# Root, column sums and turns of the identity in the first two pairs of an attention pipeline

## Chip, cores, metric

One NeuronCore of a Trainium2 chip runs the whole program. The metric is the device time of one execution in microseconds, the median of several runs. The trace is that of one profiled execution; its times count from the start of its span.

## What is computed

A batch of 32 images (3 x 128 x 128) and 32 texts (128 tokens) goes through two layers at width 256; only the first layer matters here. Cut to it:

```python
img = einsum(patches16x16(x), W) + b            # 64 image tokens per batch element
txt = take(weight, x_txt)                        # 128 text tokens
h   = concat(img, txt)                           # [32, 192, 256]
n   = layernorm(h)
q, k, v = n @ wq.T, n @ wk.T, n @ wv.T
h   = h + softmax(causal(q @ k.T / 16)) @ v
n2  = layernorm(h)
h   = h + ternary(gelu(ternary(n2, w_up)), w_down)
# ternary(x, w): x / (rms(x) + eps) times w_t.T, where w_t is sign(w) where |w| > 0.5 * mean|w|, else 0
```

The second layer (a gated linear recurrence and a mixture of eight experts) follows and is not touched.

## The kernel before

The first layer works on pairs of batch elements, 16 pairs, n = 0 to 15; a pair is 3 tiles of 128 tokens. All products are f32 made from a high part in the rounded type that TensorE takes and a low remainder, so most operands are split: ScalarE or VectorE copies the high part, VectorE or GpSimd subtracts it to get the low part. `product(..., three(...))` sums high x high, high x low and low x high. The ternary weights are exact and need no split.

The work of one pair is cut into pieces with names, and one list, `order`, gives the sequence of the pieces. Each engine walks through this same list in each step g and does the part of a piece that is its own. `offset` says which pair a piece works on in step g: pieces of offset 2 (tok, emb, root1, apply1, xT, x_split, t, t_split, score, max, and also merge and tern_up) work on pair g+2, those of offset 1 (exp, pT, v, pv, h1, scale2, x2T, also abs_down and tern_down) on pair g+1, up, gelu and down on pair g, patch_split and gather on pair g+3, patch_load on pair g+4. Steps -4 to 1 are written out before the loop, so pair 0 runs tok to max in step -2 and exp to x2T in step -1, where pair 1 runs its tok to max; the first up and down products come in step 0. Semaphores order the engines; an engine's queue is in order.

The pieces of the first half, with what each does:

- patch_split: VectorE casts `patches` to `pat_h` (`patch_hi`, for pairs 0 and 1 called from other places, for pair 1 at the end of emb of pair 0), GpSimd subtracts to `pat_l` (L333). patch_load on SyncE waits for both before it loads the next pair's patches into the single buffer.
- tok: 18 products of 256 columns from the patches and the token weights (loaded in chunks and split on the way in).
- merge (pair 0 only): folds wq and wk into one matrix; qk_split splits it.
- emb: VectorE adds the bias, takes `bn_stats` and `bn_aggr` of three tiles. root1: GpSimd adds epsilon and takes the power -0.5. apply1: VectorE norms x (L625).
- xT: six TensorE transposes; x_split: ScalarE high, VectorE low. t: 12 products of 384 columns; t_split likewise; score: 18 products of 256 columns; max: masks and takes row maxima.
- exp, pT, v (18 products), pv (15 products), h1, root2, scale2, x2T (six transposes), x2_split.

The conversion of the ternary weights runs once, inside these steps: `abs_sum(n)` sums the absolute values of the raw weights on VectorE (n = 0 up, n = 1 down), a product with a matrix of ones on TensorE sums over the partitions (its result is alpha), and `ternary(n)` scales alpha and then makes two halves of 1024 columns in two VectorE instructions each:

```python
if g == -2:
    abs_sum(0)                                   # VectorE, ahead of emb of pair 0
if kind in ("merge", "tern_down") and n == 0:    # TensorE
    pe.wait_ge(s["w_abs"], q + 1); matmul(ps[:, 7, q:q + 1], ones, absum[:, q:q + 1])
```

abs_down stands behind apply1, tern_up behind x_split, tern_down behind t_split. up of pair 0 waits for the up weights, down for the down weights.

PSUM has eight banks: XT in 0 and 1, t and the scores (and tok) in 2 and 3, v and pv in 4 and 5, up and down in 6 and 7, alpha in a column of 7. `ident` is the identity matrix, made by GpSimd before the first layer's block.

Of the kernel before, what the change touches and what calls it, by code (L numbers as in the profile page):

```python
# [18 lines left out]
ALU = mybir.AluOpType  # L19
ACT = mybir.ActivationFunctionType  # L20
F32 = mybir.dt.float32
# [5 lines left out]
P = 128  # L27
# [44 lines left out]
def part_a(nc, W, io, consts):  # L72
    with ExitStack() as ctx:
# [74 lines left out]
        for src, hi, lo in ((io["tokW"], tok_h, tok_l), (io["wvT"], wv_h, wv_l)):  # L148
            cols = flat(hi).shape[1]
            for a in range(0, cols, 1024):  # L150
# [10 lines left out]


        order = """ids_load exp gelu_table tok merge pT up.0 up.1 patch_split patch_load emb pT_split root1 gelu.0 gelu.1 v
                v_split apply1 qk_split abs_down up.2 up.3 gelu.2 add.1 up.4 pv gelu.3 add.2 xT gelu.4 up.5 x_split tern_up
                gelu.5 up.6 add.3 up.7 gelu.6 gelu.7 exp_table t h1 root2 gather t_split tern_down add.4 add.5
                down.0 down.1 score scale2 add.6 add.7 x2T down.2 max ss x2_split rscale
                h2.0 h2.1 h2.2""".split()
        order = [(w.split(".")[0], int((w + ".0").split(".")[1])) for w in order]
        offset = {"turn_win": 0, "fold": 0, "up": 0, "gelu": 0, "add": 0, "down": 0, "ss": 0, "rscale": 0, "h2": 0, "tok": 2, "emb": 2, "root1": 2, "apply1": 2,
# [117 lines left out]
        @block.gpsimd  # L287
        def _(pool):

            nc.gpsimd.memset(mask[:], 0.0).then_inc(s["mask_zero"], 1)  # L290
            pool.wait_ge(s["mask_zero"], 1)
            nc.gpsimd.affine_select(out=mask[:, 0, :], in_=mask[:, 0, :], compare_op=ALU.is_ge, fill=MASKED,
                                    base=0, pattern=[[-1, D]], channel_multiplier=1).then_inc(s["mask_zero"], 1)
            pool.wait_ge(s["mask_zero"], 2)

            nc.gpsimd.affine_select(out=mask[:, 0, 0:N_IMG], in_=mask[:, 0, 0:N_IMG], compare_op=ALU.is_ge,
                                    fill=MASKED, base=N_IMG - 1, pattern=[[0, N_IMG]],
                                    channel_multiplier=-1).then_inc(s["mask_zero"], 1)

            nc.gpsimd.memset(mask[:, 1, N_IMG:2 * N_IMG], MASKED)  # L300
            nc.gpsimd.memset(mask[:, 2, 0:N_IMG], MASKED)
            nc.gpsimd.affine_select(out=mask[:, 1:3, P:2 * P], in_=mask[:, 1:3, P:2 * P], compare_op=ALU.is_ge,
                                    fill=MASKED, base=0, pattern=[[0, 2], [-1, P]],
                                    channel_multiplier=1).then_inc(s["mask_ready"], 1)

            def gather(n, sl, half):
                pool.wait_ge(ids_in[sl], 16 * (half + 1))
                wait(pool, s["h1_done"], n - 1)
                settle(pool)
                for j in range(2):  # L310
                    pool.indirect_dma_start(
                        emb[:, sl, 1 + j, :], None, io["table"],
                        bass.IndirectOffsetOnAxis(ap=ids[:, sl, j:j + 1], axis=0),
                    ).then_inc(text_in[sl], 16)

            def prepare(g):
                if g == -4:
                    gather(0, 0, 0)

            def piece(kind, k, n, sl, half):  # L320
                if kind == "gather" and not (isinstance(n, int) and n == 0):
                    gather(n, sl, half)
                if kind == "gelu" and k in lo_pool and not (isinstance(n, int) and n == G - 1 and k in last_lo_vector):

                    if k in hi_scalar:
                        pool.wait_ge(s["ffn_hi_s"], len(hi_scalar) * n + hi_scalar.index(k) + 1)
                    else:
                        pool.wait_ge(s["ffn_hi"], (FC - len(hi_scalar)) * n + k + 1)
                    nc.gpsimd.tensor_tensor(act_l[:, k, :], act[:, k % DEEP, :], act_h[:, k, :].bitcast(F32),  # L329
                                            ALU.subtract).then_inc(s["ffn_lo"], 1)  # L330
                if kind == "patch_split":
                    pool.wait_ge(s["patch_hi"], n + 1)
                    nc.gpsimd.tensor_tensor(pat_l[:], patches[:], pat_h[:].bitcast(F32),  # L333
                                            ALU.subtract).then_inc(s["patch_lo"], 1)
                if kind == "root1":
                    pool.wait_ge(s["ln_aggr"], n + 1)
                    settle(pool)
                    nc.gpsimd.tensor_scalar(ve[:], moments[:, :, 1], LN_EPS, None, ALU.add).then_inc(s["ln_ve"], 1)
                    pool.wait_ge(s["ln_ve"], n + 1)
                    wait(pool, s["ln_out"], n)  # L340
                    nc.gpsimd.tensor_tensor(rstd[:], ve[:], halfpow[:, 1, 0:TILES], ALU.pow).then_inc(s["ln_rstd"], 1)
                if kind == "rscale":

                    pool.wait_ge(s["ms_done"], n + 1)
                    wait(pool, s["rden_done"], n)
                    nc.gpsimd.tensor_tensor(rms[:], ms[:], halfpow[:, 0, 0:TILES], ALU.pow).then_inc(s["rms_done"], 1)
                if kind == "root2":
                    pool.wait_ge(s["ln2_aggr"], n + 1)
                    settle(pool)
                    nc.gpsimd.tensor_scalar(pair[:, 0, :], moments2[:, :, 1], 0.0, None, ALU.add)  # L350
                    nc.gpsimd.tensor_scalar(pair[:, 1, :], moments2[:, :, 1], LN_EPS, None,
                                            ALU.add).then_inc(s["ln2_pair"], 1)
                    pool.wait_ge(s["ln2_pair"], n + 1)
                    nc.gpsimd.tensor_tensor(roots[:], pair[:], halfpow[:, 0:1, 0:TILES].to_broadcast([P, 2, TILES]),
                                            ALU.pow).then_inc(s["ln2_roots"], 1)

            run(pool, piece, prepare)
# [96 lines left out]
        def _(v):  # L454
# [5 lines left out]
                v.wait_ge(s["w_abs_parts"], n + 1)  # L460
                nc.vector.tensor_reduce(absum[:, n:n + 1], abparts[:], AX_X, ALU.add).then_inc(s["w_abs"], 1)

            def ternary(n):
                raw, out = raw_tern[n], tern[n][2]
                v.wait_ge(s["w_alpha_ps"], n + 1)
                nc.vector.tensor_scalar(half_alpha[:, n:n + 1], ps[:, 7, n:n + 1], 0.5 / (D * FF), None,
                                        ALU.mult).then_inc(s["w_alpha"], 1)
                v.wait_ge(s["w_alpha"], n + 1)

                for part in range(2):  # L470
                    col = slice(1024 * part, 1024 * part + 1024)
                    k = 2 * n + part
                    wait(v, s["w_sum"], k)
                    nc.vector.tensor_scalar(tern_tmp, raw[:, col], -1.0, half_alpha[:, n:n + 1], ALU.mult,
                                            ALU.is_gt).then_inc(s["w_sign"], 1)
                    v.wait_ge(s["w_sign"], k + 1)
                    last = nc.vector.scalar_tensor_tensor(out=out[:, col], in0=raw[:, col],
                                                          scalar=half_alpha[:, n:n + 1], in1=tern_tmp,
                                                          op0=ALU.is_gt, op1=ALU.subtract)
                    last.then_inc(s["w_sum"], 1)  # L480

            def softplus_arg():
                omega = vec[:, 0, :]
# [29 lines left out]
            def prepare(g):  # L513
# [6 lines left out]
                for n in chunks_of.get(g, ()):  # L520
                    chunk_lo(n)
                if g == -2:
                    abs_sum(0)
                    v.wait_ge(s["const_in"], 16)
                    v.wait_ge(s["mask_ready"], 1)

# [15 lines left out]
            def piece(kind, k, n, sl, half):  # L542
# [24 lines left out]
                    nc.vector.tensor_tensor(sqsum[:], sqsum[:], sq[:, k % DEEP, :], ALU.add).then_inc(s["sqsum_done"], 1)  # L567
                if kind == "x_split":
                    lo(xT_l[:], XT[:, :, 0:GT], xT_h[:].bitcast(F32), s["x_hi"], s["x_lo"], n)
                if kind == "t_split":  # L570
                    lo(tT_l[:], ps[:, 2:4, 0:GT], tT_h[:].bitcast(F32), s["t_hi"], s["t_lo"], n)
                if kind == "v_split":
# [16 lines left out]
                if kind == "abs_down" and isinstance(n, int) and n == 0:  # L589
                    abs_sum(1)  # L590
                if kind in ("tern_up", "tern_down") and isinstance(n, int) and n == 0:
                    ternary(("tern_up", "tern_down").index(kind))
                if kind == "max":
                    v.wait_ge(s["score_done"], n + 1)
                    wait(v, s["pT_done"], n)
# [86 lines left out]
        def _(pe):  # L682
# [16 lines left out]
            def keys(x, k, i):  # L699
# [2 lines left out]
                    return x[:, k, 0:2 * P]  # L702
                return x[:, k, :].rearrange("p (t c) -> p t c", t=TILES)[:, 0:3:2, :]

            def piece(kind, k, n, sl, half):
                if kind == "merge" and isinstance(n, int) and n == 0:
                    pe.wait_ge(s["qk_in"], 32)
                    for m in range(DC):
# [1 line left out]
                            last = nc.tensor.matmul(MERGED[:, m, :], wq[:, c, m * P:(m + 1) * P], wk[:, c, :],  # L710
                                                    start=(c == 0), stop=(c == DC - 1))
                    last.then_inc(s["merge_ps"], 1)
                if kind in ("merge", "tern_down") and isinstance(n, int) and n == 0:
                    q = ("merge", "tern_down").index(kind)
                    pe.wait_ge(s["w_abs"], q + 1)
                    nc.tensor.matmul(ps[:, 7, q:q + 1], ones[:], absum[:, q:q + 1], start=True,
                                     stop=True).then_inc(s["w_alpha_ps"], 1)
# [962 lines left out]
```

## Time and profile before

| | |
|---|---|
| median of 3 runs | 1002.25 us (1001.86 to 1004.44) |
| profiled execution | 1003.52 us, its span 1001.5 us |
| TensorE busy | 932.3 us (93%) |
| VectorE busy | 786.3 us (79%) |
| ScalarE busy | 594.7 us (59%) |
| GpSimd busy | 542.3 us (54%) |
| mean granted TensorE clock | 0.974 |

The span is what the profile covers; the execution's own time is 2.0 us longer. In the profile PE is TensorE's matrix products, PEld its weight loads, DVE VectorE, ACT ScalarE, POOL GpSimd and SP SyncE. An instruction's row names the line of the kernel, the output and the inputs. Several products of a form that follow each other stand in one row with their count. Matrix products overlap in their pipeline, so each one's duration is longer than the distance to the next. The granted clock (PEclk) is a share of the full 2.4 GHz: 1.00 or 0.50.

### The profile page before, as it was taken

The numbers are of one execution on the slowest core, as the hardware profiler recorded it, in microseconds if no ns is written. First come the engines' busy times: TensorE is split into PE (matmuls) and PEld (weight loads), VectorE is DVE, ScalarE is ACT, GpSimd is POOL, SyncE is SP. The second block draws the span as 40 slices with busy tenths as digits, with TensorE's granted clock in tenths as the row PEclk, the third lists the DMA queues.
The fourth block names the chain that finished last, engine by engine and source line by source line (L and its number), as shares of the span: only waits on it lengthen the run. The fifth ranks groups of instructions, "written<-read, shape, count | busy, mean of one in ns | idle before, by whom it ended". The sixth has DMA issues, their size and how long they took to land. (4 is left out here: it accounts for less than half of the span.)

```text
span 1001.5 us, 19582 instructions
## 1 busy us (share of the span) xinstructions
PE 932.3 (93%) x5896; PEld 834.9 (83%) x5896; DVE 786.3 (79%) x2396; ACT 594.7 (59%) x1181; POOL 542.3 (54%) x662
## 2 busy tenths in 40 slices
PE   3779999999999999988799999999998999997998
PEld 2679999999999999875588888888887788886887
DVE  3578777777777777774399999999997888996776
ACT  1246666666666666664566677767664676652541
POOL 4136666666666666443445555445443446542663
PEclk9679999999999999999899999999999899999999
DMA  6001111111111113003699999999999999994210
GB/s 214 22 27 44 43 44 35 50 36 47 39 45 34 50 33 148 17 17 111 79 149 155 157 155 154 156 155 155 153 153 177 146 151 150 140 143 78 102 63 22
DMA packets 135877, 96.33 MB, mean 96 GB/s; under 512 B 12270, under 2 KB 130166, under 8 KB 135158
## 3 DMA queue, kind: packets, MB, share of 16 engines
q1 hardware_dynamic: 134262, 91.20, 53.0%
q0 software_dynamic: 1536, 4.20, 1.4%
q8 instruction: 35, 0.57, 0.3%
q14 instruction: 44, 0.36, 0.2%
HBM read 31.91 MB, written 13.11 MB: 45 GB/s over the span
## 5 line engine op out<-in xcount | busy, mean ns | idle before, releaser
L329 POOL TENSOR_TENSOR gelu_lo<-gelu_out,gelu_hi 128x384 fp32r<-128x384 f32 x124 | 145.4, 1200 | 30.0 <-DVE gelu_hi L548 28.7
L1025 POOL TENSOR_TENSOR B_y<-B_scan_in,B_states 128x512 f32<-128x512 f32 x48 | 61.9, 1289 | 97.9 <-ACT B_states L1099 97.9
L741 PE MATMUL psAB<-ternary_down,gelu_hi 128*128 128x256 f32 x384 | 96.6, 290 | 4.8 <-POOL gelu_lo L329 3.9
L685 PE MATMUL psAB<-x2T_hi,ternary_up 128*128 128x384 f32 x256 | 93.2, 364 | 2.5 <-DVE residual L675 2.3
L741 PE MATMUL psAB<-ternary_down,gelu_lo 128*128 128x256 f32 x384 | 93.3, 282 | 0.0
L685 PE MATMUL psAB<-x2T_lo,ternary_up 128*128 128x384 f32 x256 | 86.2, 337 | 0.0
L1273 PE MATMUL psAB<-Win_hi,B_x_hi 128*128 128x512 f32 x192 | 83.5, 435 | 0.0
L1285 PEld LDWEIGHTS psAB<-B_partial_dots,B_minus_same_batch 128*128 128x128 f32 x384 | 65.3, 191 | 17.9 <-DVE B_partial_dots L1176 8.9
L741 PEld LDWEIGHTS psAB<-ternary_down,gelu_hi 128*128 128x128 f32 x384 | 72.2, 188 | 8.8 <-POOL gelu_lo L329 7.5
L1192 DVE SCALAR_TENSOR_TENSOR psAB<-B_decayed_u,psAB 128x128 f32<-128x128 f32 x192 | 67.9, 354 | 13.4 <-PE psAB L1285 12.1
L1273 PE MATMUL psAB<-Win_hi,B_x_lo 128*128 128x512 f32 x192 | 75.7, 394 | 0.0
L1273 PE MATMUL psAB<-Win_lo,B_x_hi 128*128 128x512 f32 x192 | 75.1, 391 | 0.0
L1037 POOL TENSOR_TENSOR B_decayed_u<-B_scan_in 128x512 f32<-128x512 f32 x48 | 62.0, 1292 | 24.2 <-DMA B_scan_in<-B_stage 14.0
L741 PEld LDWEIGHTS psAB<-ternary_down,gelu_lo 128*128 128x128 f32 x384 | 72.4, 189 | 0.0
L1031 POOL TENSOR_TENSOR B_v_scale<-B_half_vv,half_powers 128x1 f32<-128x1 f32 x48 | 26.3, 548 | 83.6 <-ACT B_v_squared L1120 77.5
L1176 DVE CUSTOM_DVE_ANT_0 B_products<-B_scan_in,psAB 128x128 f32<-128x128 f32 x192 | 55.1, 287 | 18.7 <-DVE psAB L1192 7.8
L398 ACT ACTIVATE gelu_out<-psAB 128x384 f32<-128x384 f32 x128 | 62.8, 491 | 10.9 <-PE psAB L685 10.3
L333 POOL TENSOR_TENSOR patches_lo<-patches,patches_hi 128x768 fp32r<-128x768 f32 x16 | 29.5, 1847 | 65.7 <-DVE patches_hi L536 65.6
L1181 DVE TENSOR_TENSOR psAB<-psAB,B_scan_in 128x128 f32<-128x128 f32 x192 | 57.5, 299 | 6.5
L567 DVE TENSOR_TENSOR gelu_sq_sum<-gelu_sq_sum,gelu_sq 128x384 f32<-128x384 f32 x105 | 61.2, 583 | 1.7
L1285 PE MATMUL psAB<-B_partial_dots,B_minus_same_batch 128*128 128x1 f32 x384 | 55.0, 212 | 7.0 <-DVE B_partial_dots L1176 6.8
L685 PEld LDWEIGHTS psAB<-x2T_hi,ternary_up 128*128 128x128 f32 x256 | 48.0, 188 | 11.8 <-ACT gelu_out L398 7.7
(265 smaller groups left out, 3345.2 us busy)
## 6 DMA issues: line engine op xcount, KB each, us to landing
B_scan_in<-B_stage SPq DMA_DIRECT2D x192, 256.0 KB, 6.6
patches<-in_patches SPq DMA_DIRECT2D x16, 384.0 KB, 3.1
B_residual<-layer_out SPq DMA_DIRECT2D x48, 128.0 KB, 3.6
out_dram<-B_residual SPq DMA_DIRECT2D x48, 128.0 KB, 2.9
layer_out<-residual SPq DMA_DIRECT2D x32, 128.0 KB, 1.8
raw_Win<-in_experts SPq DMA_DIRECT2D x4, 768.0 KB, 4.4
raw_Wl<-in_experts SPq DMA_DIRECT2D x4, 768.0 KB, 4.2
layer_out<-residual SPq DMA_DIRECT2D x32, 64.0 KB, 1.9
```

What stands on the lines that cost most here:

```text
L329: nc.gpsimd.tensor_tensor(act_l[:, k, :], act[:, k % DEEP, :], act_h[:, k, :].bitcast(F32), ALU.subtract).then_inc(s["ffn_lo"], 1)
L398: nc.scalar.activation(act[:, k % DEEP, :], ps[:, 6 + k % 2, 0:GT], ACT.Gelu).then_inc(s["gelu_done"], 1)
L567: nc.vector.tensor_tensor(sqsum[:], sqsum[:], sq[:, k % DEEP, :], ALU.add).then_inc(s["sqsum_done"], 1)
L685: last = nc.tensor.matmul(out, a, b, start=(n == 0), stop=(n == len(terms) - 1))
L741: last = nc.tensor.matmul(ps[:, 6 + k // 2, (k % 2) * D:(k % 2 + 1) * D], x[:, c, k * P:(k + 1) * P], dn_w[:, c, :], start=(c == 0 and x i ...
L1025: nc.gpsimd.tensor_tensor(y[:, j % 2], ring[:, j % R_RING, :, GATE, :], hs[:, j % 2], ALU.mult).then_inc(s["y"], 1)
L1037: nc.gpsimd.tensor_tensor(lu[:, j % 2], ring[:, j % R_RING, :, LAM, :], ring[:, j % R_RING, :, U, :], ALU.mult).then_inc(s["lu"], 1)
L1176: nc.vector.tensor_tensor_reduce(prod[:], ring[:, j % R_RING, k, U, :], previous(j, k), 1.0, 0.0, ALU.mult, ALU.add, part[:, t % 2:t % 2 + ...
L1181: nc.vector.tensor_tensor(state(j, k), state(j, k), ring[:, j % R_RING, k, DRIVE, :], ALU.subtract).then_inc(s["scan"], 1)
L1192: nc.vector.scalar_tensor_tensor(out=state(i, k), in0=lu[:, i % 2, k, :], scalar=dot[:, t % 2:t % 2 + 1], in1=state(i, k), op0=ALU.mult, o ...
L1273: last = nc.tensor.matmul(out, a, b, start=(not biased and ks[0] == 0 and n == 0), stop=(ks[-1] == DC - 1 and n == len(terms) - 1), skip_g ...
L1285: nc.tensor.matmul(dot[:, t % 2:t % 2 + 1], minus[:], part[:, t % 2:t % 2 + 1], start=True, stop=True).then_inc(s["dot"], 1)
```

## The change

It touches the first pairs only.

- On GpSimd the low part of pair 1's patches moves from the piece patch_split to behind the root of pair 0.
- On VectorE `abs_sum(0)` moves from the start of step -2 to behind x_split of pair 0, and TensorE's alpha product for the up weights from merge to t_split, in front of which it waits for the column sums.
- `ternary` makes one half per call. The halves are tern_up.0 behind t_split, tern_up.1 behind max, tern_down.0 and tern_down.1 behind t_split in their step.
- TensorE transposes the identity into PSUM bank 6, which nobody reads then, a number of times ahead of the wait of eight pieces: 110 times in all. A piece's turns stand before all that the piece does on TensorE, its waits included.

```diff
-                v_split apply1 qk_split abs_down up.2 up.3 gelu.2 add.1 up.4 pv gelu.3 add.2 xT gelu.4 up.5 x_split tern_up
-                gelu.5 up.6 add.3 up.7 gelu.6 gelu.7 exp_table t h1 root2 gather t_split tern_down add.4 add.5
-                down.0 down.1 score scale2 add.6 add.7 x2T down.2 max ss x2_split rscale
+                v_split apply1 qk_split abs_down up.2 up.3 gelu.2 add.1 up.4 pv gelu.3 add.2 xT gelu.4 up.5 x_split
+                gelu.5 up.6 add.3 up.7 gelu.6 gelu.7 exp_table t h1 root2 gather t_split tern_up.0 tern_down.0 tern_down.1 add.4 add.5
+                down.0 down.1 score scale2 add.6 add.7 x2T down.2 max tern_up.1 ss x2_split rscale
...
+            def patch_lo(n):
+                pool.wait_ge(s["patch_hi"], n + 1)
+                nc.gpsimd.tensor_tensor(pat_l[:], patches[:], pat_h[:].bitcast(F32),
+                                        ALU.subtract).then_inc(s["patch_lo"], 1)
...
-                if kind == "patch_split":
-                    pool.wait_ge(s["patch_hi"], n + 1)
-                    nc.gpsimd.tensor_tensor(pat_l[:], patches[:], pat_h[:].bitcast(F32),
-                                            ALU.subtract).then_inc(s["patch_lo"], 1)
+                if kind == "patch_split" and not (isinstance(n, int) and n == 1):
+                    patch_lo(n)
...
                     nc.gpsimd.tensor_tensor(rstd[:], ve[:], halfpow[:, 1, 0:TILES], ALU.pow).then_inc(s["ln_rstd"], 1)
+                    if isinstance(n, int) and n == 0:
+                        patch_lo(1)
...
-            def ternary(n):
+            def ternary(n, part):
...
                 if g == -2:
-                    abs_sum(0)
...
                 if kind == "x_split":
                     lo(xT_l[:], XT[:, :, 0:GT], xT_h[:].bitcast(F32), s["x_hi"], s["x_lo"], n)
+                    if isinstance(n, int) and n == 0:
+                        abs_sum(0)
...
+            fill = {("tok", 0): 40, ("xT", 0): 16, ("t", 0): 10, ("score", 0): 10, ("pv", 0): 10, ("xT", 1): 4,
+                    ("t", 1): 10, ("score", 1): 10}
+
             def piece(kind, k, n, sl, half):
+                if isinstance(n, int):
+                    for _ in range(fill.get((kind, n), 0)):
+                        nc.tensor.transpose(ps[:, 6, 0:P], ident[:], ident[:])
...
-                if kind in ("merge", "tern_down") and isinstance(n, int) and n == 0:
-                    q = ("merge", "tern_down").index(kind)
+                if kind in ("t_split", "tern_down") and isinstance(n, int) and n == 0 and k == 0:
+                    q = ("t_split", "tern_down").index(kind)
```

## Rows read from the trace of the kernel before

**Rows 1.** The page, granted TensorE clock in 40 slices of 25 us, in tenths.

```profile
PEclk9679999999999999999899999999999899999999
```

**Rows 2.** Windows over the run: length, each engine's busy us and instructions, PEclk, DMA.

```profile
0.00:100.00 100.00, 70.19 (x418) 66.57 (x419) 62.41 (x150) 38.20 (x75) 41.40 (x53) 0.83 0.23 77
100.00:200.00 100.00, 99.04 (x734) 95.86 (x733) 78.45 (x224) 64.69 (x136) 69.38 (x68) 1.00 0.15 43
```

**Rows 3.** What TensorE waited for, 0 to 70 us: total, times, longest.

```profile
PE psAB L685 <- DVE tokW_lo L530: 10.9, 1, 10.9
PE psAB L696 <- DVE x_normed L625: 6.3, 1, 6.3
PE psAB L685 <- DVE xT_lo L540: 3.8, 2, 1.9
PE psAB L685 <- DVE tT_lo L540: 3.6, 2, 1.9
PE psAB L685 <- DVE v_lo L540: 2.0, 1, 2.0
```

**Rows 4.** Windows, L685's products alone: tok(0), t(0), score(0), tok(1), v(0), t(1) twice.

```profile
10.90:15.10 4.20, 4.18 (x18) 1.00 1.03 430
26.90:31.20 4.30, 4.21 (x12) 0.50 0.00 0
33.00:37.30 4.30, 4.21 (x18) 0.50 0.00 0
38.60:42.65 4.05, 3.96 (x18) 0.50 0.01 4
43.00:45.50 2.50, 2.29 (x18) 1.00 0.00 0
51.90:52.85 0.95, 0.89 (x5) 1.00 0.00 0
52.85:55.50 2.65, 2.59 (x9) 0.50 0.00 0
```

**Rows 5.** Windows, all engines: PE, PEld, DVE, ACT, POOL, PEclk, DMA.

```profile
22.10:22.30 0.20, 0.00 (x0) 0.00 (x0) 0.00 (x0) 0.00 (x0) 0.20 (x1) 0.58 0.10 31
...
49.50:52.90 3.40, 1.51 (x11) 1.27 (x10) 3.04 (x6) 2.30 (x3) 0.00 (x0) 0.99 0.00 0
...
63.20:66.50 3.30, 3.23 (x15) 3.23 (x16) 2.02 (x9) 1.65 (x5) 0.00 (x0) 0.50 0.00 0
```

**Rows 6.** Timeline, VectorE and GpSimd, 14 to 23.5 us: start, us, instruction, idle before.

```profile
14.27 2.29 DVE L458 TENSOR_REDUCE abs_sum_parts<-raw_Wl 128x32 f32<-128x2048 f32 x1 [3.51 <-DMA raw_Wl<-in_upT]
...
16.71 0.42 DVE L607 TENSOR_TENSOR embedded<-psAB,patch_bias 128x256 f32<-128x256 f32 x1
...
18.65 0.53 DVE L536 CAST patches_hi<-patches 128x768 fp32r<-128x768 f32 x1
19.25 1.80 POOL L333 TENSOR_TENSOR patches_lo<-patches,patches_hi 128x768 fp32r<-128x768 f32 x1 [10.18 <-DVE patches_hi L536]
...
21.47 0.90 POOL L341 TENSOR_TENSOR ln_rstd<-ln_var_eps,half_powers 128x3 f32<-128x3 f32 x1
22.41 1.06 DVE L625 TENSOR_SCALAR x_normed<-embedded,ln_moments,ln_rstd 128x256 f32<-128x256 f32 x3 [3.23 <-POOL ln_rstd L341]
```

**Rows 7.** Tile patches, 0 to 20 us: its two loads, issued at 2.4 and 9.1.

```profile
DMA to landing us min/median/max: 3.2/5.9/8.6
```

**Rows 8.** Timeline, VectorE, 56 to 63.5 us.

```profile
56.32 0.96 DVE L540 TENSOR_TENSOR tT_lo<-psAB,tT_hi 128x768 fp32r<-128x768 f32 x1 [1.70 <-ACT tT_hi L374]
...
60.56 1.28 DVE L477 SCALAR_TENSOR_TENSOR ternary_down<-raw_Wv,half_alpha,gelu_sq 128x1024 fp32r<-128x1024 f32 x1
...
62.16 1.06 DVE L668 TENSOR_SCALAR x_normed<-residual,ln_moments,ln_scale 128x256 f32<-128x256 f32 x3
```

**Rows 9.** Timeline, TensorE: the six transposes of xT(0) and of xT(1).

```profile
23.52 1.54 PE L696 MATMUL psAB<-ident,x_normed 128*128 128x128 f32 x6 [6.31 <-DVE x_normed L625]
...
49.25 0.82 PE L696 MATMUL psAB<-ident,x_normed 128*128 128x128 f32 x6
```

More of the change, by code:

```diff
@@ L461, in abs_sum @@
                 nc.vector.tensor_reduce(absum[:, n:n + 1], abparts[:], AX_X, ALU.add).then_inc(s["w_abs"], 1)
-            def ternary(n):
+            def ternary(n, part):
                 raw, out = raw_tern[n], tern[n][2]
[L465 to L480, printed above, removed]
+                if part == 0:
+                    v.wait_ge(s["w_alpha_ps"], n + 1)
+                    nc.vector.tensor_scalar(half_alpha[:, n:n + 1], ps[:, 7, n:n + 1], 0.5 / (D * FF), None,
+                                            ALU.mult).then_inc(s["w_alpha"], 1)
+                    v.wait_ge(s["w_alpha"], n + 1)
+                col = slice(1024 * part, 1024 * part + 1024)
+                k = 2 * n + part
+                wait(v, s["w_sum"], k)
+                nc.vector.tensor_scalar(tern_tmp, raw[:, col], -1.0, half_alpha[:, n:n + 1], ALU.mult,
+                                        ALU.is_gt).then_inc(s["w_sign"], 1)
+                v.wait_ge(s["w_sign"], k + 1)
+                nc.vector.scalar_tensor_tensor(out=out[:, col], in0=raw[:, col], scalar=half_alpha[:, n:n + 1],
+                                               in1=tern_tmp, op0=ALU.is_gt, op1=ALU.subtract).then_inc(s["w_sum"], 1)
             def softplus_arg():
@@ L591, in piece @@
                 if kind in ("tern_up", "tern_down") and isinstance(n, int) and n == 0:
-                    ternary(("tern_up", "tern_down").index(kind))
+                    ternary(("tern_up", "tern_down").index(kind), k)
                 if kind == "max":
```

## The prediction

> **What bounds the kernel now.** I read four views, from coarse to fine. The forty slices of the page show TensorE's granted clock near full almost everywhere, and low in the second and third slice [rows 1]. The windows over the run say the same in time: after 100 us TensorE is busy 99 of 100 us at the full clock, in the first 100 us it is busy 70 us at a mean of 0.83 [rows 2]. So behind the first steps the kernel is bound by TensorE, and what the first steps save should arrive at the end one for one: nothing else paces the loop, and the loop's own work isn't changed. TensorE's waits in the first 70 us name the chain of the first two pairs: 10.9 us for the low part of the token weights, 6.3 for the first normed x, 3.8 and 3.6 for the low parts of xT and tT of both pairs [rows 3]. These are steps that follow each other with nothing to put between.
>
> The fourth view is the clock inside this head. The engine has two levels, 1.2 and 2.4 GHz. The same eighteen 256-wide products take 4.2 us in the score of pair 0, and 2.29 us in v of pair 0 [rows 4], a ratio of 0.54. The clock column says 1.00 for tok of pair 0, yet its duration (4.18 us for eighteen) is that of half clock: before the first recorded change I go by durations. The column then shows a fall at 22.2 us, after TensorE had stood idle since 17 (its 6.3 us ahead of xT at 23.5 [rows 3]); half clock through t and score of pair 0 and through tok of pair 1; full clock from 42.6; half again from 52.9, after a stretch in which it was busy only 1.5 of 3.4 us; and a return in 66.5, at the end of 3.2 us without a pause [rows 4, 5]. t and score of pair 0 are each 4.2 us of unbroken products, with 1.8 us between them, and did not raise it.
>
> **The change, part by part.**
>
> *Root ahead of the split, column sums behind x's split.* In the kernel before, VectorE holds the patch-bias add until 16.71 us, because it sums the columns of the raw ternary weights from 14.27 on for 2.3 us and a short second reduction follows; the product it needs was ready at 15.1 [rows 4, 6]. Then the statistics end at about 18.65, VectorE casts the patches of pair 1 (0.53 us), and GpSimd first takes their low part from 19.25 to 21.05. Only then does the variance go to the root: 0.90 us from 21.47, and x is normed from 22.41 [rows 6].
> After the change the add starts when tok is done: 15.1 at half clock, 13.3 if tok runs at full clock. Statistics take 1.94 us as before (16.71 to 18.65), so they end at 17.1 or 15.3. The variance add and root then need 1.4 us (from 21.05 to 22.4), so rstd is there at 18.5 or 16.7. But the cast of the patches of pair 1 stays ahead of x's norming on VectorE, and their load was issued at 9.1 and landed 8.6 us later, at 17.7 [rows 7], behind the weights. Nothing in the change moves that load. So the cast ends at about 18.3, and norming starts at 18.3 to 18.5 at either clock: **-4.0 us** (-3.9 to -4.1). The queue behind the cast is VectorE's; on GpSimd the low split and the gather of pair 1 now follow the root, at about 20.1 instead of 21.05, and the load of the next patches goes out that much earlier, so nothing waits longer.
>
> *The column sums' new place.* Behind xT's low part they take 2.3 + 0.2 us of VectorE. The next thing it owes is tT's low part, which waits for t (4.2 us at half, 2.3 at full clock) and for ScalarE's copy: of the 1.8 us from t's end to the score's start the low part itself is 0.96 [rows 4, 8], so the copy some 0.8. Cover 3.1 us at the least, cost 0. If the cover were gone it would be up to 2.5. The alpha product on TensorE now waits for them after t: they end 2.6 us after xT's low part, t at full clock 2.3 us after it, and 1.8 us of wait follow anyway: cost 0.
>
> *Ternary halves.* In pair 1 the two halves of the down weights stand between tT's low part (ends 57.28) and 61.84, so a half is 2.3 us with its gaps and its share of the scaling [rows 8]. The first up half takes as much of VectorE between tT's low part and the row maxima; the score covers it with 2.3 us at full clock plus its start and end: cost **+0.1**. The second stands after the maxima, under tok of pair 1: 0. The down halves keep their place. Behind them the second norm goes from 62.16 to 63.22: from 56.3 on that stretch is VectorE's, so a faster score of pair 1 gives **0**.
>
> *The identity turns.* A 128-wide transpose of f32 takes (1.54 - 0.48)/5 = 0.21 us at half and (0.82 - 0.27)/5 = 0.11 us at full clock, where 0.48 and 0.27 are what one takes by itself, an estimate; six of them are 1.54 and 0.82 [rows 9]. The 40 ahead of tok: 8.5 us at the most, inside the 10.9 us of wait. 16 ahead of xT(0): 1.8 to 3.4 us, from about 15 on, ready before 19.4. 10 ahead of t, score and pv: 1.1 us at full clock in waits of 1.9, 1.8 and 2.0: free; at half clock 2.1, and with the alpha product in front score(0) and score(1) come 0.6 us late each. The 4 ahead of xT(1) stand in no wait: pv(0) runs until 49.25, where xT(1) starts at once [rows 9], so they cost **+0.4** (0.9 at half).
>
> What they give is the clock, if they raise it. This is the step I can't read off a row, so I bound it. Nothing: the clock rises as products alone make it. Everything: full clock from before tok(0) to the end of the head. Then xT(0) 1.54 to 0.82: **-0.7**; t(0) 4.2 to 2.3: **-1.9**; score(0) the same: **-1.9**; tok(1) 3.96 to 2.29: **-1.7** (v of pair 0 and pv were at full clock already); t(1) 0.89 + 2.59 to 2.3: **-1.2**; x2T the same 0.7 as xT, and 0.3 of tok(2), whose rest I take as hidden under the exponentials of pair 1: **-1.0** [rows 4, 9].
> Do transposes wake the clock? The row that bears on it is 63.2 to 66.5: it begins with the six transposes of x2T (1.1 us of the 3.2), and the clock rose at its end, while 4.2 us of products with a pause behind them did not raise it [rows 4, 5]. So I take it that they count nearly like products. The Trainium skill says otherwise (TensorE: Matmul & The Clock Gate, Part 4: PE-mode transpose): by it the full clock doesn't engage for transposes, since they don't count as busy in the same way. The trace speaks against it, with that one stretch. By the rule the sum would be that of the second rival.
>
> Sum with the full clock throughout: -4.0 - 0.7 - 1.9 - 1.9 - 1.7 - 1.2 - 1.0 + 0.1 + 0.4 = **-11.9**. It won't be throughout. Between the 16 turns (done by about 16.7) and xT at 19.4 TensorE stands still for 2.7 us, and a longer still stretch from 17 made it fall before: I give back xT's 0.7 and a third of t, +1.3. Between score(1), which ends near 60 at full clock, and x2T at 63.3 on the old scale lie 3.3 us without a turn: I give back the last term, +1.0. Likeliest: -11.9 + 2.3 = **-9.6 us**.
>
> The sum was made on the profiled execution (span 1001.5, 1003.5 with 2.0 around it), which is 1.3 us above the median of 1002.25. The same saving from the median: 1002.25 - 9.6 = **992.6 us**; a profile after should have a span near 992.
>
> **The rivals.**
> 1. *Clock up throughout*: 1002.25 - 11.9 = 990.4. For it: the waits are filled densely. Against: the two unfilled ones above.
> 2. *Transposes don't wake the clock.* Only the root's part is left, and the turns run at half clock: -4.0 + 0.6 + 0.6 + 0.4 + 0.1 = -2.3, so 999.9. Against it speaks the stretch at 63.2.
> 3. *The clock falls in the gap ahead of xT(0) and comes back only in tok(1).* Then xT(0), t(0), score(0) and half of tok(1) stay at half clock, the turns of the score cost 0.6: of -11.9 + 1.0 are lost 0.7 + 1.9 + 1.9 + 0.9 + 0.6 = 6.0; left is -4.9, so 997.3. For it: VectorE's wait for the patches makes this gap, and the fall at 22.2 is a precedent; against: 10 turns fill the wait right behind xT.
> 4. *No change*: a head start that the loop doesn't keep, because its first steps wait for something with its own time, a gather or a load: 1002. Against: both are issued earlier too, and after 100 us TensorE is 99% busy.
> 5. *Slower.* The rise at 42.6 is lost: it came out of 4.0 us of tok(1) [rows 4]. If the turns neither raise the clock nor keep it and tok(1) starts at another moment, v(0), pv(0) and xT(1) run at half clock too: +1.9, +1.6, +0.7, t(1)'s first half +0.5, the four turns +0.5 more, pv's turns +0.2; on -2.3 that is +3.1, so 1005.4. It decides only if transposes count for nothing and this rise is missed as well.
>
> **How the numbers follow.** Forecast 0.55, rival 1 0.11, rival 3 0.15, rival 2 0.12, rival 4 0.05, rival 5 0.02. 0.3% is 3.0 us, about what this measurement can tell from no change. The forecast and rivals 1 and 3 are faster beyond it (0.81); rival 2 at -2.3 us lies just inside, with 0.05 of its 0.12 beyond: faster 0.86, the same 0.07 + 0.05 = 0.12, slower 0.02. The range goes from 989.0, 1.4 under rival 1 for its rounded terms, to 998.5, 1.2 over rival 3: it leaves out rivals 2, 4 and 5, 0.19.
>
> **What the profile after would show.** The patch-bias add at 13.3 (15.1 if the 40 turns didn't raise the clock), VectorE idle ahead of the cast of pair 1's patches until 17.7 with a DMA as releaser, norming at 18.3. Score(0)'s eighteen products in 2.3 us and not 4.2. Norming of pair 1 some 9 us earlier, x2T near 54, the products of the first ternary layer starting near 58.5. A short low of the granted clock around 18 to 23 us and another near 52. The prediction is wrong if products behind the turns last as long as at half clock, if norming waits for something later than the patches, or if TensorE shows new waits between 60 and 100 us.

## The result and the profile after

| | before | after |
|---|---|---|
| median of 9 runs each | 1004.44 us (1001.56 to 1007.69) | 995.29 us (992.05 to 999.17) |
| ratio | | 0.9916, 95% interval 0.9898 to 0.9935 |
| profiled execution, its span | 1003.52 us, 1001.5 us | 999.17 us, 997.4 us |

The change makes the kernel 0.84% faster by the ratio, which is 8.4 us (the two medians lie 9.2 apart). The prediction was 992.6 us (989.0 to 998.5), 9.6 us less than the median it started from. The profiled execution after is the slowest of its nine, and its span is only 4.1 us shorter; where the other half went is read further down.

The windows over the run of the kernel after, with the columns of [rows 2]:

```profile
0.00:100.00 100.00, 83.92 (x580) 79.67 (x581) 70.02 (x165) 45.00 (x89) 48.95 (x61) 0.97 0.23 77
100.00:200.00 100.00, 99.20 (x736) 96.06 (x735) 78.87 (x224) 64.70 (x135) 68.94 (x67) 1.00 0.15 43
```

TensorE's mean clock in the first 100 us is 0.97 where it was 0.83 (the column reads 1.00 ahead of the first recorded change in both, so both means are somewhat high); the loop behind it is as it was. TensorE's waits of 0 to 70 us, which answer to [rows 3]:

```profile
PE psAB L699 <- DVE x_normed L628: 4.6, 1, 4.6
PE psAB L699 <- DVE x_normed L671: 3.2, 1, 3.2
...
PE psAB L688 <- DVE tokW_lo L531: 1.6, 1, 1.6
PE psAB L688 <- DVE tT_lo L541: 1.0, 2, 0.6
PE psAB L688 <- DVE v_lo L541: 0.9, 1, 0.9
PE psAB L688 <- DVE xT_lo L541: 0.8, 1, 0.8
```

The waits that have turns in them shrank, though the work behind them starts no earlier for that. Two are long: 4.6 us ahead of xT(0), and 3.2 us ahead of x2T(0), which was 1.7 and now has the end of a faster score in front of it.

The windows of the products alone (columns of [rows 4]) are tok(0), t(0), score(0), tok(1), t(1), score(1) and tok(2):

```profile
10.90:13.35 2.45, 2.39 (x18) 1.00 1.01 413
24.70:27.20 2.50, 2.38 (x12) 0.97 0.02 3
29.00:31.50 2.50, 2.42 (x18) 1.00 0.00 0
32.80:35.30 2.50, 2.38 (x18) 1.00 0.00 0
...
44.90:47.35 2.45, 2.38 (x12) 1.00 0.00 0
49.10:51.65 2.55, 2.41 (x18) 1.00 0.00 0
55.90:59.70 3.80, 3.71 (x18) 0.60 0.00 0
```

All five blocks that ran wholly or partly at half clock in [rows 4] take 2.4 us now, as at full clock; score(1), which has no row there, is too. tok(2), which has none either, is at 0.60: the clock fell at 55.5, just behind the wait of 3.2 us, and came back at 59.0.

TensorE's transposes in time, the turns (L716, out psAB, in ident) and xT's (L699); [rows 9] are those of before:

```profile
2.00 7.37 PE L716 MATMUL psAB<-ident 128*128 128x128 f32 x40 [2.00 <-PEq L1609]
...
14.88 1.91 PE L716 MATMUL psAB<-ident 128*128 128x128 f32 x16
21.35 1.51 PE L699 MATMUL psAB<-ident,x_normed 128*128 128x128 f32 x6 [4.55 <-DVE x_normed L628]
22.66 2.32 PE L716 MATMUL psAB<-ident 128*128 128x128 f32 x10
...
41.76 0.60 PE L716 MATMUL psAB<-ident 128*128 128x128 f32 x4
42.20 0.82 PE L699 MATMUL psAB<-ident,x_normed 128*128 128x128 f32 x6
```

The 40 turns take 7.37 us: all at half clock would be 8.5, all at full 4.5, so the clock rose among them, and tok(0) behind them ran at full clock. The windows say roughly when: 26 turns in the 5.4 us up to 7.4, then 15 (with those that reach in) in 1.8 us. Turn by turn the trace has them 0.21 us apart up to the one that starts at 7.8, and 0.11 apart from there on.

```profile
2.00:7.40 5.40, 5.40 (x26) 5.40 (x27) 0.75 (x1) 1.27 (x2) 4.20 (x9) 1.00 0.70 223
...
7.60:9.40 1.80, 1.76 (x15) 1.52 (x13) 0.95 (x1) 0.92 (x2) 1.49 (x1) 1.00 0.99 351
```

TensorE had done nothing but turns of the identity until then. Transposes wake the clock in this kernel. (The Trainium skill, TensorE: Matmul & The Clock Gate, Part 4: PE-mode transpose, says that they don't; the trace differs, and the measurement decides.) The clock column itself says 1.00 from the start here as in the kernel before, so the distances between instructions show this rise and the column doesn't.

VectorE and GpSimd, 13 to 21 us, which answer to [rows 6]:

```profile
13.46 0.42 DVE L610 TENSOR_TENSOR embedded<-psAB,patch_bias 128x256 f32<-128x256 f32 x1 [2.68 <-PE psAB L688]
...
18.25 0.56 DVE L537 CAST patches_hi<-patches 128x768 fp32r<-128x768 f32 x1 [2.77 <-DMA patches<-in_patches]
18.73 2.56 DVE L628 TENSOR_SCALAR x_normed<-embedded,ln_moments,ln_rstd 128x256 f32<-128x256 f32 x3
...
16.00 0.90 POOL L344 TENSOR_TENSOR ln_rstd<-ln_var_eps,half_powers 128x3 f32<-128x3 f32 x1
18.89 1.91 POOL L318 TENSOR_TENSOR patches_lo<-patches,patches_hi 128x768 fp32r<-128x768 f32 x1 [1.99 <-DVE patches_hi L537]
```

The add starts at 13.46 (predicted 13.3), the root is ready at 16.9 (16.7), VectorE waits 2.77 us for the load of pair 1's patches as foretold, and norming starts at 18.73 (18.3), because the load landed 9.1 us after its issue here and not 8.6 as before. But norming takes 2.56 us instead of 1.06. Its three instructions, in the view of the tile (ns, min/median/max):

```profile
L628 DVE TENSOR_SCALAR x_normed<-embedded,ln_moments,ln_rstd x3: 409/426/1893, 18.7 to 20.9; 128x256 f32<-128x256 f32 x3
```

The one of 1893 ns started behind GpSimd's low part (18.89 to 20.80) and ended 0.15 us behind its end: VectorE stood inside an instruction, which no view of waits shows.

**Where the profile's other 4 us are.** up of pair 0 starts at 59.98 instead of 68.07, so the head gained 8.1 us in the profiled execution too. At pT of pair 15 the lead is still there, 409.80 instead of 417.98. In both executions two stalls of 1.2 and 0.6 us stand there (the kernel after):

```profile
409.80 0.74 PE L826 MATMUL psAB<-ident,probs 128*128 128x128 f32 x5 [1.21 <-DVE x2T_lo L541]
411.16 0.69 PE L688 MATMUL psAB<-x2T_hi,ternary_up 128*128 128x384 f32 x1 [0.62 <-DVE residual L678]
411.65 0.52 PE L688 MATMUL psAB<-x2T_lo,ternary_up 128*128 128x384 f32 x1
```

Behind them the products are 0.32 us apart, as at half clock; in the kernel before they are 0.17 apart behind the same stalls. The windows of the kernel after:

```profile
407.00:412.00 5.00, 3.17 (x23) 2.87 (x22) 3.66 (x14) 3.66 (x9) 0.85 (x1) 0.85 0.00 0
412.00:417.00 5.00, 5.00 (x22) 5.00 (x21) 1.13 (x4) 1.39 (x3) 2.01 (x2) 0.50 0.28 80
417.00:422.00 5.00, 5.00 (x35) 4.77 (x34) 3.38 (x6) 3.19 (x7) 1.78 (x2) 0.96 0.00 0
...
432.00:442.00 10.00, 8.35 (x48) 7.63 (x47) 5.88 (x21) 4.04 (x8) 1.85 (x2) 0.83 0.21 40
```

At 434.7 the lead is down to 5.3 us and at the end of this layer, with the second low (0.83), to 3.9. The kernel before had neither low in its profiled execution; of the ten experiments three had one at pT of pair 15 (2, 8 and 9), one the later one (6), and six neither. So the spans of one pair of profiled executions can't weigh this change. The medians can, and the head (from the start to up of pair 0) does it to about 1 us either way: experiment 6 has the change's head and reached up of pair 0 at 60.53, and experiment 10, with four turns fewer, at 58.02.

### The profile page after: what moved, and what is told of

Read it like the earlier page. It is cut to its first block and busy times, and to the rows that moved or that the text cites. A ratio compares the mean times of both kernels' runs of the same rounds, so it can differ in the third digit from the quotient of the medians.

```text
span 997.4 us, 19802 instructions
## 1 busy us (share of the span) xinstructions
PE 942.3 (94%) x6006; PEld 844.9 (85%) x6006; DVE 785.9 (79%) x2396; ACT 594.5 (60%) x1181; POOL 542.2 (54%) x662
## 5 line engine op out<-in xcount | busy, mean ns | idle before, releaser
L403 ACT ACTIVATE gelu_out<-psAB 128x384 f32<-128x384 f32 x128 | 62.6, 489 | 13.6 <-PE psAB L688 13.3
L1309 PE MATMUL psAB<-Wout_hi,B_y_hi 128*128 128x256 f32 x192 | 55.3, 288 | 2.7 <-DVE B_y_lo L1245 1.5
```

The costliest lines, as they stand in the source:

```text
L403: nc.scalar.activation(act[:, k % DEEP, :], ps[:, 6 + k % 2, 0:GT], ACT.Gelu).then_inc(s["gelu_done"], 1)
```

## The experiments

The first seven give a ratio to the kernel before on the same chip; the last three ran once each. With each stands the time at which up of pair 0 starts in its profile (68.07 before, 59.98 after).

**1. No turns.** The changed order alone.

```diff
-            fill = {("tok", 0): 40, ("xT", 0): 16, ("t", 0): 10, ("score", 0): 10, ("pv", 0): 10, ("xT", 1): 4,
-                    ("t", 1): 10, ("score", 1): 10}
+            fill = {}
```

> The changed kernel without its 110 turns of the identity; the order of the work stays changed. If the turns carry the gain through the clock, as I hold: the first products of tok run at half clock again (eighteen in 4.2 us), norming starts near 18.7, score(0) takes 4.2 us, and of the 8.4 us gained some 2 to 3 are left: about 0.998 of the kernel before, the first ternary product (up of pair 0) near 65.5. If the order carries it and the turns only accompany it: up of pair 0 near 61 and 0.993 or less.

Measured: 1000.61 us, ratio 0.9976 (0.9964 to 0.9988); up of pair 0 at 64.48; tok(0) back at 4.17 us; norming from 18.98, 2.57 long. The order is worth 2.4 us. The clock rises in places here too, by products alone (0.56, 0.65 and 0.66 in the windows of t(0), score(0) and tok(1)), so the head is earlier than the time says; the time is what was expected, the place of up near it.

**2. Turns only.** The kernel before with the same `fill` and its loop.

> The kernel before with the turns alone; root, low part, column sums and ternary halves stand as before. By the clock theory: the norm of x still starts at 22.4 (nothing of that chain is TensorE's: the add waits for the column sums until 16.7), and then t, score and tok(1) run at full clock: up of pair 0 near 62, 0.994 of before. By the rival that turns do not wake the clock: 1.000 or above.

Measured: 998.37 us, ratio 0.9955 (0.9937 to 0.9974); up of pair 0 at 62.58. Norming starts at 21.79: TensorE is done with tok early, but the add waits for the column sums until 16.08. The turns are worth 4.5 us on the old order. 2.4 and 4.5 make 6.9 of the 8.4; the intervals (1.2, 1.9 and 1.9 us to each side) leave open whether the two help each other.

**3. The low part behind norming.** In the kernel after, one wait more on GpSimd.

```diff
                     if isinstance(n, int) and n == 0:
+                        pool.wait_ge(s["ln_out"], 1)
                         patch_lo(1)
```

> The changed kernel with one wait more: GpSimd takes the low part of the patches of pair 1 only when x of pair 0 is normed. In the profile after, norming took 2.56 us and not 1.06, its middle instruction 1.9 us, while GpSimd ran that low part. If the two hold each other off: norming 1.06 again, xT(0) at 19.9 instead of 21.35, 1.5 us less in the head, 0.990 of before. If something else is slow there (the cast's data, the DMA's writes): norming stays at 2.5 and nothing is gained.

Measured: 996.11 us, ratio 0.9919 (0.9899 to 0.9939), no gain over the change that its times could show; up of pair 0 at 57.56, 2.4 us earlier than in the kernel after. Some 0.7 of that is norming's earlier start, since the load of the patches landed 8.3 us after its issue here. VectorE and GpSimd:

```profile
18.07 1.06 DVE L629 TENSOR_SCALAR x_normed<-embedded,ln_moments,ln_rstd 128x256 f32<-128x256 f32 x3
...
19.65 1.94 DVE L532 TENSOR_TENSOR wv_lo<-weight_stage,wv_hi 128x512 fp32r<-128x512 f32 x1
21.51 0.94 DVE L542 TENSOR_TENSOR xT_lo<-psAB,xT_hi 128x768 fp32r<-128x768 f32 x1
...
19.21 1.83 POOL L318 TENSOR_TENSOR patches_lo<-patches,patches_hi 128x768 fp32r<-128x768 f32 x1 [1.17 <-DVE x_normed L629]
```

The mechanism is shown: norming is 1.06 again once GpSimd is quiet. But the block moved on to the low part of wv, which started behind GpSimd's and took 1.94 instead of 0.68 us, until 0.55 us after GpSimd was done at 21.04, and xT's low part started behind it. The instruction before, qk_lo, which reads one operand from PSUM, started 0.16 us ahead of GpSimd's and ran beside it for 0.5 us; neither got longer (0.68 and 1.83 us). (The Trainium skill, SBUF — State Buffer, Who interferes with whom, says that VectorE and GpSimd share a pair of ports, that a VectorE instruction in a two-port mode, or one with two SBUF inputs beside a GpSimd instruction that reads SBUF, excludes it and is excluded by it, and that the second to start blocks fully. The row of wv_lo agrees; in which mode norming ran no view shows.)

Between the two profiled executions the shorter head isn't lost: this one leads the kernel after by 2.4 us at up of pair 0 and by 2.4 us at the end of the span. Against the kernel before each of them lost some 4 us in between, the kernel after in the two lows above, this one in the second layer, where its clock was low from 909.8 to 920.0. The windows, TensorE alone:

```profile
910.00:915.00 5.00, 1.68 (x8) 0.50 0.14 47
915.00:920.00 5.00, 5.00 (x26) 0.50 0.49 157
```

The kernel after has 1.00 and 0.91 in these two windows, its own low there being from 919.1 to 922.5. Why the median of six doesn't move stays open; the mean granted clock of those six executions lies between 0.983 and 0.988, as wide as the nine of the kernel after.

**4. Norming first.** `patch_hi(1)` moves from the end of emb of pair 0 to the end of apply1 of pair 0.

> The changed kernel with VectorE's cast of the patches of pair 1 behind the norming of pair 0, so that norming no longer waits for their load, and GpSimd's low part comes after it by itself. If the load (landed at 17.7) was the limit, as predicted: norming at 16.95, 1.06 long, xT(0) near 18.1 instead of 21.35, 3.2 us less in the head: 0.988 of before. The gap of TensorE ahead of xT(0) shrinks as well, so the clock should stay up. Rival: the head is then set by something else, such as the wait of the folded weights' low part (qk_lo): a gain under 1 us.

Measured: 993.2 us, ratio 0.9898 (0.9878 to 0.9917); up of pair 0 at 57.75. Norming starts at 17.88 with 1.45 us of wait for the root, no longer for the load, and is 1.06 long; xT(0) at 19.0 instead of 21.35. Norming was to start at 16.95 and xT(0) at 18.1: tok(0) ran partly at half clock here (0.64 over its window). The clock had risen early in the 40 turns, these were over by 8.1 us, and behind the wait of 2.83 us that followed it fell again at 12.1. The same fall is there in the profiles of experiments 3, 6 and 10, with waits of 2.81, 3.05 and 2.80 us between turns and tok(0), and absent in those of the kernel after and of experiments 2, 5 and 7, with 1.57, 1.62, 2.25 and 0.66. wv's low part took 1.93 us here as well. By the point estimates that is 1.8 us better than the change, with intervals that overlap.

**5. Turns ahead of x2T(0).** `("x2T", 0): 24` added to `fill`.

> The changed kernel with 24 more turns of the identity, ahead of x2T of pair 0, where TensorE stood idle 3.25 us in the profile after and the clock then fell (the products of tok(2) ran at half clock, 0.21 us apart). 24 turns take 2.6 us at full clock and fit. If that dip costs what the prediction gave back for it: tok(2) at full clock, up of pair 0 some 0.8 to 1.0 us earlier for the same start of norming, 0.991 of before. If the exponentials of pair 1 bound that place anyway: up of pair 0 no earlier.

Measured: 994.45 us, ratio 0.9911 (0.9888 to 0.9934); from x2T(0) to up of pair 0 3.80 us instead of 5.13.

```profile
52.04 2.78 PE L716 MATMUL psAB<-ident 128*128 128x128 f32 x24
55.44 0.87 PE L699 MATMUL psAB<-ident,x_normed 128*128 128x128 f32 x6 [0.62 <-DVE x_normed L671]
56.56 0.36 PE L688 MATMUL psAB<-tokW_hi,patches_hi 128*128 128x256 f32 x1 [0.25 <-DVE row_max L601]
56.76 0.28 PE L688 MATMUL psAB<-tokW_lo,patches_hi 128*128 128x256 f32 x1
```

tok(2)'s products are 0.12 us apart and the low is gone. On this stretch that is 1.3 us, more than the 1.0 given back for it. Up of pair 0 starts at 59.24, only 0.7 earlier than in the kernel after, because here the low ahead of xT(0) lasted through most of t(0); in the times the gain doesn't stand out.

**6. Turns late.** The kernel after with ten turns into bank 4 in front of pT of pair 15.

```diff
+                if isinstance(n, int) and n == G - 1 and kind == "pT":
+                    for _ in range(10):
+                        nc.tensor.transpose(ps[:, 4, 0:P], ident[:], ident[:])
```

> The changed kernel with 10 turns (into PSUM bank 4) ahead of the wait of pT of pair 15, where in the profile after the clock fell at 410 us and again at 438 us, and the lead of 8.1 us that up of pair 0 had shrank to 3.9. If those two falls are chance (where the stalls of 1.2 and 0.6 us lie against the clock's own steps), the profile after is a slow one of its kind and the median gains by this about half of one such fall, 1 to 1.5 us: 0.990. If the lead is lost for another reason, the last steps still shrink it with the clock at full.

Measured: 996.59 us, ratio 0.9931 (0.9909 to 0.9954): no gain; up of pair 0 at 60.53. The low at this place is absent in its profile, but the next one (0.83 in the window 430 to 440) is there, and without such turns the low at pT of pair 15 is there in four of ten profiled executions (the kernel after, experiments 2, 8 and 9) and absent in six. That these lows come by chance fits all of it; that ten turns remove them isn't shown.

**7. All together.** Norming first; wv's low part behind the column sums; 52 turns ahead of tok(0), none ahead of xT(1), 24 ahead of x2T(0), the ten of experiment 6.

> All together: norming ahead of the cast, the low part of wv behind the column sums (in the profile with norming first it took 1.93 us and not 0.68, while GpSimd ran the low part of the patches, and held xT's low part), 52 turns ahead of tok instead of 40, none ahead of xT(1), 24 ahead of x2T(0), 10 ahead of pT of pair 15. Against 0.990 with norming first alone: 0.6 for wv, 0.4 for the four turns, 0.9 for x2T, 0 to 1.8 for tok, 1 for pT: 0.987, up of pair 0 near 55. By the rival that turns cost as they gain: no better than norming first, 0.990.

Measured: 988.16 us, ratio 0.9848 (0.9823 to 0.9873); up of pair 0 at 54.22. Window and VectorE of this kernel:

```profile
0.00:100.00 100.00, 89.95 (x660) 85.57 (x661) 73.33 (x178) 45.88 (x90) 52.56 (x64) 1.00 0.24 80
...
16.94 1.06 DVE L626 TENSOR_SCALAR x_normed<-embedded,ln_moments,ln_rstd 128x256 f32<-128x256 f32 x3 [1.45 <-POOL ln_rstd L344]
18.67 0.56 DVE L537 CAST patches_hi<-patches 128x768 fp32r<-128x768 f32 x1 [0.68 <-DMA patches<-in_patches]
19.15 0.68 DVE L587 SCALAR_TENSOR_TENSOR qk_lo<-psAB,qk_hi 128x512 fp32r<-128x512 f32 x1
19.81 0.96 DVE L541 TENSOR_TENSOR xT_lo<-psAB,xT_hi 128x768 fp32r<-128x768 f32 x1
```

Norming at 16.94, where the arithmetic of experiment 4 had it; xT's low part 1.7 us earlier than in experiment 3, 1.1 of it by norming's start and 0.6 by what stands between the two; no low clock in the head once it had risen among the turns ahead of tok(0). This version beats both kernels, and its interval lies wholly below the change's.

**8, 9, 10: one run each.** In 8 the kernel before with the root alone moved; in 9 the sums alone (without turns, the root behind the low part as before); in 10 the kernel after without the four turns ahead of xT(1). One run is read for its steps here, and its time shows no difference of this size.

> The kernel before with only the root ahead of the low part of pair 1's patches, no turns, column sums where they were. Statistics end at 18.65 as before, root until 20.1, norming from 20.15; GpSimd starts the low part at the same moment, so norming takes 2.5 and not 1.06 us, if the two hold each other off: xT(0) near 22.7 against 23.52. If they do not: xT(0) at 21.3.

1002.72 us (before 1002.52); up of pair 0 at 66.48. Norming from 20.36, 2.57 us long, one instruction of 1903 ns, xT(0) at 22.99 instead of 23.52. The root's new place alone earns 2.05 us and loses 1.5 at once to the low part that now runs beside norming.

> The kernel before with only the column sums, their alpha product and the ternary halves moved; no turns, the root behind the low part as before. The add starts at 15.1, statistics end at 17.1, the cast waits for its patches until 17.7 and ends at 18.3, low part until 20.1, root until 21.4: norming at 21.45 and 1.06 long, xT(0) near 22.6 against 23.52. The t chain is not delayed by the sums: t(0)'s low part follows its ScalarE copy without idle of its own.

```profile
15.23 0.42 DVE L608 TENSOR_TENSOR embedded<-psAB,patch_bias 128x256 f32<-128x256 f32 x1 [4.47 <-PE psAB L686]
...
18.30 0.56 DVE L535 CAST patches_hi<-patches 128x768 fp32r<-128x768 f32 x1 [1.04 <-DMA patches<-in_patches]
22.09 1.06 DVE L626 TENSOR_SCALAR x_normed<-embedded,ln_moments,ln_rstd 128x256 f32<-128x256 f32 x3 [3.23 <-POOL ln_rstd L344]
...
31.73 0.96 DVE L539 TENSOR_TENSOR tT_lo<-psAB,tT_hi 128x768 fp32r<-128x768 f32 x1 [2.73 <-ACT tT_hi L377]
```

1006.04 us (one run of the kernel before beside it: 1008.53); up of pair 0 at 66.76. Norming at 22.09, 0.3 us earlier than before and not 1.0: the add is 1.5 us earlier, and the load of the patches, which landed 9.2 us after its issue, takes it back. tT's low part waits 2.73 us for ScalarE's copy with the sums long done, so they hold nothing up.

> The changed kernel without the four turns ahead of xT of pair 1. By the prediction they stand in no wait and cost 0.4 us: xT(1) follows the last product of pv at once (0.12 us after its start) instead of 0.56 us after it, and t(1) starts 0.4 us earlier. If xT(1) waits for the normed x anyway, nothing moves.

xT(1) starts at 40.55, 0.12 us behind the start of pv's last product at 40.43 (41.64 and 42.20 in the kernel after). The four turns cost 0.44 us. Its one time was 989.9 us (the same run of the kernel before beside it); up of pair 0 at 58.02.

## Why the prediction was right, and where it was off

The time lay inside the range and near the forecast: 8.4 us by the ratio, 9.6 foretold. Step by step, with starts in the two profiled executions (before, after):

| from, to | before | after | measured | foretold |
|---|---|---|---|---|
| start to norming of x(0) | 22.41 | 18.73 | -3.7 | -4.0 |
| norming to xT(0) | 1.11 | 2.62 | +1.5 | 0 |
| xT(0) to t(0) | 3.44 | 3.40 | 0 | -0.7, given back |
| t(0) to score(0) | 6.10 | 4.28 | -1.8 | -1.9, 0.6 given back |
| score(0) to tok(1) | 5.63 | 3.84 | -1.8 | -1.9 + 0.1 |
| tok(1) to xT(1) | 10.56 | 9.33 | -1.2 | -1.7 + 0.4 |
| xT(1) to t(1) | 2.71 | 2.71 | 0 | 0 |
| t(1) to score(1) | 5.37 | 4.28 | -1.1 | -1.2 |
| score(1) to x2T(0) | 5.94 | 5.66 | -0.3 | 0 |
| x2T(0) to up of pair 0 | 4.80 | 5.13 | +0.3 | -1.0, given back |
| sum, to up of pair 0 | 68.07 | 59.98 | -8.1 | -9.6 |

- *That transposes wake the clock* was read off one stretch of 3.2 us. It held: the 40 turns raised it alone, and without turns 6 of the 8.4 us go (experiment 1). Rival 2 falls, and rival 5 with it.
- *The load of pair 1's patches as the new limit of norming* held: VectorE waits 2.77 us for it, and with norming first the wait is gone (experiments 4 and 7). That the change doesn't move it was right too, but its time from issue to landing differs from execution to execution, from 7.9 to 9.5 us over the runs; 9.1 in this one is why norming's start gained 3.7 and not 4.0.
- *The column sums at no cost and the ternary halves at 0.1 us* held as far as the rows of the table tell: VectorE waits 0.90 us for ScalarE's copy between the sums and tT's low part.
- *Four turns ahead of xT(1): +0.4* held, 0.44 (experiment 10).
- *The two lows* came in this execution behind the two waits where they were expected, some 3 us later than the times named, at 21.4 to 24.8 and 55.5 to 59.0. The first ended as t(0) began, so the third of t's saving that was given back was kept. Neither is fixed: experiment 4 had one inside tok(0) and none ahead of xT(0), experiment 7 none. That the two fell where the prediction had them is in part luck. Rival 1, no low, and rival 3, a low that lasts into tok(1), would be other draws of the same thing; no profiled execution with the change's turns showed either. Rival 4 falls with up of pair 0 and the medians.
- *What was missed* is the term for norming, "-4.0 us (-3.9 to -4.1)" up to its start and nothing behind it. The low part of the patches was moved to run beside norming, and I costed it only by who waits for it. It costs 1.5 us (2.56 instead of 1.06), shown by experiments 3 and 8. That one term is as large as the difference between the head's -9.6 and -8.1; the other rows are off by up to 0.5 us either way and cancel. The median's agreement within 1.2 us is no finer test than that, since the medians of the kernel before on record differ by 2.2 us among themselves (1002.25 for three runs, 1004.44 for nine).

What stays open: how often the late lows come, and what decides where they fall. The remainder behind up of pair 0 lay between 930.1 and 937.4 us over the ten experiments, without an order by kernel, which hides differences of 1 to 2 us.

## What to carry to other kernels

Where the first steps are a chain of short operations, look at the distance between equal products before you look at their count: here the half clock cost more (4.5 us by experiment 2) than the order of the instructions (2.4 by experiment 1). Idle matrix time in front of a wait can be filled with transposes of the identity that nobody reads, if they end before the wait does but not long before it (experiment 4). When a piece of GpSimd's is moved, ask what VectorE runs at that moment, not only who waits for the result; and when one limit goes, name the next (here a load) and ask whether the order lets it matter. Compare kernels like this by a time inside the trace as well as by medians, since where the clock falls differs from execution to execution; the time inside the trace has its own scatter, about 1 us either way here.

## What the runs showed of the hardware

- Transposes alone raised the clock: 40 turns of the identity in 7.37 us instead of 8.5 (an estimate from the distance at half clock), with the change of distance at 7.8 us, after 5.8 us of turns.
- A VectorE instruction can be held inside its own duration by GpSimd: 1893 and 1903 ns (the kernel after, experiment 8) for one that takes 409, 1.94 us (experiment 3) for one that takes 0.68, with no wait shown, each time one that started behind GpSimd's. With one operand in PSUM and a start 0.16 us ahead of GpSimd's (qk_lo, experiment 3) it took its 0.68 us.
- The clock column says 1.00 ahead of the first change on record, while the products in it ran at half clock (4.18 us for eighteen).
- Behind the same stalls of 1.2 and 0.6 us the clock fell in one execution and not in another: 0.32 or 0.17 us between the products behind them.
